# A two-layer decoder on one core: in both cross attentions the first eight heads' values and softmax denominators made by one product, and the first batches' expert slots counted on GpSimd

## The reference, cut to what matters

```python
x = x + L0_attn(layernorm(x))                          # banded self attention
x = x + L0_xattn(layernorm(x), ctx, ctx)               # cross attention, biases    <- changed
x = x + L0_ffn(layernorm(x))                           # 8 experts, top 2
x = x + L1_attn(layernorm(x) * gamma + beta)           # self attention, heads of 64
x = x + L1_xattn(ctx, ctx, layernorm(x))               # cross attention            <- changed
x = x + L1_ffn(layernorm(x))                           # 8 experts, top 2

# a cross attention, per batch and head:
scores = q @ k.T * scale          # 256 x 77
attn = softmax(scores, axis=-1)
out = attn @ v                    # 256 x 16
y = concat_heads(out) @ wo.T + bo
```

## Time and profile before

| | |
|---|---|
| median of 3 runs | 1504.77 us (1500.16 to 1508.09) |
| profiled execution | 1504.03 us, span 1502.4 us |
| granted TensorE clock, mean | 0.993 |
| TensorE busy | 1433.9 us, 95% of the span |
| VectorE busy | 748.7 us, 50% |
| ScalarE busy | 619.1 us, 41% |
| GpSimd busy | 490.5 us, 33% |
| stretch of L0x / L1x units | about 226 to 356 us / 1078 to 1213 us |

### The profile page before, as it was taken

The page is one execution under the profiler, slowest core; times in us unless marked ns, Lnnn a source line. Parts: engine busy times, 40 slices in busy tenths (PEclk is TensorE's granted clock), DMA queues, the critical chain, the costliest instruction groups (busy, mean ns, idle before and its releaser), DMA issues. The chain is left out here.

```text
span 1502.4 us, 34667 instructions
## 1 busy us (share of the span) xinstructions
PE 1433.9 (95%) x11880; PEld 1159.7 (77%) x11881; DVE 748.7 (50%) x2160; ACT 619.1 (41%) x1711; POOL 490.5 (33%) x758
## 2 busy tenths in 40 slices
PE   7999998988999999999999999999899899999998
PEld 5676766767899999976777777777666579999997
DVE  6666757887433333344444444444278862222222
ACT  2433346653222222235445444545366533333332
POOL 3545442444322122223233233333224452222222
PEclk9999999999999999999999999999999999999999
DMA  9920000152243434120000000000001522533332
GB/s 316 333 69 2 2 2 9 45 176 62 50 119 67 144 71 114 32 64 1 0 1 1 1 1 1 1 1 0 1 16 44 174 78 40 149 93 94 94 90 34
DMA packets 79666, 97.46 MB, mean 65 GB/s; under 512 B 10523, under 2 KB 72579, under 8 KB 79555
## 3 DMA queue, kind: packets, MB, share of 16 engines
q1 hardware_dynamic: 64643, 77.58, 16.4%
q0 software_dynamic: 13680, 17.19, 6.6%
q10 hardware_dynamic: 1232, 1.18, 0.2%
HBM read 57.51 MB, written 39.59 MB: 65 GB/s over the span
## 5 line engine op out<-in xcount | busy, mean ns | idle before, releaser
L1741 POOL TENSOR_TENSOR L1a_prob<-L1a_prob,L1a_rtot 128x1024 f32<-128x1024 f32 x64 | 121.1, 1892 | 275.8 <-DVE L1a_rtot L1614 275.8
L2270 PEld LDWEIGHTS L0x_ps<-L0f_rows_t,L0f_w_up 128*128 128x128 f32 x1584 | 183.7, 193 | 10.4 <-issue 9.0
L2270 PE MATMUL L0x_ps<-L0f_rows_t,L0f_w_up 128*128 128x128 f32 x1584 | 185.8, 277 | 5.6 <-issue 4.8
L2346 ACT ACTIVATE L1f_hid<-L1x_ps,L1f_b_up 128x128 f32<-128x128 f32 x296 | 92.4, 363 | 163.0 <-PE L1x_ps L2270 159.7
L2270 PEld LDWEIGHTS L1x_ps<-L1f_rows_t,L1f_w_up 128*128 128x128 f32 x1184 | 139.5, 194 | 3.4 <-issue 1.6
L2270 PE MATMUL L1x_ps<-L1f_rows_t,L1f_w_up 128*128 128x128 f32 x1184 | 140.4, 277 | 0.6 <-ACT L1f_rows_t L2330 0.6
L2279 PE MATMUL L1x_ps<-L1f_w_down,L1f_hid 128*128 128x256 f32 x592 | 134.1, 380 | 1.9 <-issue 1.9
L2214 POOL TENSOR_TENSOR turn<-eps 128x1 f32<-128x1 f32 x74 | 13.6, 184 | 372.3 <-DVE wv L2448 367.7
L1683 ACT ACTIVATE L1a_prob<-L1a_ps_s,L1a_nmax 128x256 f32<-128x256 f32 x256 | 118.2, 473 | 38.1 <-DVE L1a_nmax L1609 38.1
L2279 PEld LDWEIGHTS L1x_ps<-L1f_w_down,L1f_hid 128*128 128x128 f32 x592 | 109.6, 190 | 15.5 <-issue 2.1
L1245 POOL TENSOR_SCALAR_AFFINE_SELECT L0a_prob<-L0a_prob 128x128 f32<-128x128 f32 (+1 forms) x256 | 79.8, 353 | 104.3 <-ACT L0a_prob L1199 104.3
(11 more groups left out here) (486 smaller groups left out, 2812.5 us busy)
## 6 DMA issues: line engine op xcount, KB each, us to landing
expert_table<-zero SPq DMA_DIRECT2D x1, 16640.0 KB, 68.5
L0f_w_up<-in_w_dram SPq DMA_DIRECT2D x8, 1408.0 KB, 6.8
L1f_w_up<-in_w_dram SPq DMA_DIRECT2D x8, 1024.0 KB
L1f_w_down<-in_w_dram SPq DMA_DIRECT2D x8, 1024.0 KB
L0f_w_down<-in_w_dram SPq DMA_DIRECT2D x8, 768.0 KB, 8.7
L1f_rows<-expert_table SPq DMA_DIRECT2D x35, 130.0 KB
L0f_rows<-expert_table SPq DMA_DIRECT2D x32, 130.0 KB
sums<-X SPq DMA_DIRECT2D x8, 256.0 KB
```

Source lines behind the costliest of these rows:

```text
L1741: eng.tensor_tensor(v, v, r.unsqueeze(2).to_broadcast([P, 2 * QT_N, S]), ALU.mult).then_inc(norm_done, 1)
L2270: ins = eng.matmul(ps_h[c][:, o:o + P], w_up[par][:, t, w0:w0 + P], rows_t[:, t, :], start=(t == 0), stop=(t == DT - 1))
L2346: ins = eng.activation(hid[:, c, k * P:(k + 1) * P], ps_h[c][:, k * P:(k + 1) * P], ACT.Gelu, bias=b_up[par][:, 2 * c + k:2 * c + k + 1])
```

## The change

In both cross attentions:

- The tile v_s of an even unit (heads 0 to 7) now holds a value in every even column and a one in every odd column, so one product of 32 columns gives a head's values and its denominator in alternate rows. Each half of the heads goes to its own half of ps_o. Odd units (heads 8 to 15) keep two sets of products, with zeros in place of the ones and half_ones laid out to match.
- The even unit's ps_o is copied to SBUF by ScalarE (`gather`, tile gathered). SyncE brings rows together by four transfers within SBUF a batch (`move`: two for the sums, then two for the values). VectorE takes the reciprocal in SBUF (`sums_first`) and GpSimd multiplies (`first_outputs`).
- `slots` is split: `gates` stays on VectorE, the rest of the first five batches goes to GpSimd, written as `slots` there; the last three batches keep the old `slots` on VectorE.
- VectorE's `sums` of the odd unit runs ahead of the ordering of the experts, and waits of odds, choose and send are adapted.
- The first two weight loads are issued by ScalarE, one at the end of unit 11, one at the end of unit 12, and no longer by SyncE.
- Weights wo and bias bv are permuted on the host to the new order of rows.

```diff
             b = t[1]
-            eng.wait_ge(v_cleared, b % 2 + 1)
+            eng.wait_ge(v_cleared, 2 * (b % 2 + 1))
...
-            ins = eng.activation(even_odd(v_s[b % 2][0:SC, :, :]), bank[0:SC, 0:D].rearrange("p (a two d) -> p a two d", two=2, d=DH), ACT.Copy)
+            ins = eng.activation(v_s[b % 2][0:SC, :, 0::2], bank[0:SC, 0:D].rearrange("p (h d) -> p h d", d=DH), ACT.Copy)
...
+                def move(b):
+                    eng.wait_ge(copied, b + 1)
+                    if b:
+                        eng.wait_ge(rsum_done, b)
+                    for w in range(HALVES):
+                        eng.dma_start(summed_t[1 - w::2, :], gathered[w::2, w, :]).then_inc(sums_moved, 16)
+                    if b:
+                        eng.wait_ge(first_out, b)
+                    for w in range(HALVES):
+                        eng.dma_start(valued_t[1 - w::2, :], gathered[1 - w::2, w, :]).then_inc(values_moved, 16)
+
+                move(0)
                 for b in range(B):
+                    if b + 1 < B:
+                        move(b + 1)
                     eng.wait_ge(added, b + 1)
...
-                    if b == ORDER_BY + 1:
-                        experts["first_loads"](eng)
...
+                def sums_first(b):
+                    eng.wait_ge(sums_moved, 32 * (b + 1))
+                    if b:
+                        eng.wait_ge(first_out, b)
+                    eng.reciprocal(rsum_first[:, :], summed_t[:, :]).then_inc(rsum_done, 1)
...
                     if c == 0:
+                        if b:
+                            sums_first(b - 1)
                         if b + 2 < B:
                             first["statistics"](eng, b + 2)
                         if b >= 3:
-                            slots(b - 3)
+                            gates(b - 3)
+                        if b:
+                            sums(u - 1)
+                        if b >= 3:
+                            if b == 3 and not final or b - 3 == ORDER_BY or b - 3 in FULL_BY:
+                                eng.wait_ge(slot_done, b - 2)
...
-                    if u and u < units - 1:
-                        sums(u - 1)
...
+                def gather(b):
+                    eng.wait_ge(values_done, CHUNKS * b + 1)
...
+                    eng.activation(gathered, ps_o[:, :].rearrange("p (w s) -> p w s", w=HALVES), ACT.Copy).then_inc(copied, 1)
...
                     for r in range(GROUPS):
                         exponential(u, r)
+                    if c == 1:
+                        gather(b)
...
+                    for e in range(2):
+                        if u == 2 * (ORDER_BY + 3) + 1 + e:
+                            experts["first_load"](eng, e)
...
+                def first_outputs(b):
+                    eng.wait_ge(values_moved, 32 * (b + 1))
+                    eng.wait_ge(rsum_done, b + 1)
+                    if b:
+                        eng.wait_ge(projected, b)
+                    eng.tensor_tensor(o_t[:, 0, :], valued_t, rsum_first, ALU.mult).then_inc(first_out, 1)
...
                     if c == 0:
+                        if b:
+                            first_outputs(b - 1)
                         if b + 2 < B:
                             first["spread_norm"](eng, b + 2)
                         if b >= 3:
+                            slots(b - 3)
                             send(b - 3)
...
-                    if u:
-                        eng.wait_ge(o_out, u)
-                    for summed in range(2):
+                    flat = v_s[b % 2][0:SC, :, :].rearrange("p h n -> p (h n)")
+                    if c == 1:
+                        eng.wait_ge(copied, b + 1)
+                    elif b:
+                        eng.wait_ge(o_out, b)
+                    for summed in range(c + 1):
                         for w in range(HALVES):
                             for r in range(GROUPS):
-                                lhs = half_ones[0:SC, w, :] if summed else v_s[b % 2][0:SC, c * 8 + 2 * r + 1 - w, :]
+                                o = (summed if c else w) * S
+                                n = 2 * DH * (c * 8 + 2 * r + 1 - w) - (1 - w)
+                                lhs = half_ones[0:SC, w, :] if summed else flat[:, n:n + 2 * DH]
```

More of the change, by code:

```diff
@@ L138, in batches_of @@
         return b0, b1, b1 - b0
-    def even_odd(v):
-        return v.rearrange("p (a two) (half d) -> p a (two half) d", two=2, half=2)[:, :, 0::3, :]
     def weights_in(eng):
@@ L579, in _ @@
                             choose(b - 2)
-                        if u == units - 1:
-                            sums(u - 1)
                         if b >= 1:
                             add(b - 1)
-                    if u and u < units - 1:
-                        sums(u - 1)
                 slots(B - 3)
+                sums_first(B - 1)
                 x["take_early"](0)
```

77 lines of the change are left out of this document (56 added, 21 removed).

## The result

The changed kernel takes 1526.76 us (median of 3 runs, 1525.22 to 1527.20) against 1504.77: ratio 1.0147, 95% interval 1.0102 to 1.0191. It is slower by 22 us where 8.0 us less were forecast. Two views of the profiled execution come first: the head of its page, and three lines of its lists of instructions and transfers.

A forecast was written before the change was run, and what follows sets the result against it. TensorE was taken as the bound in most batches, with VectorE and the chain behind it stepping in at a few waits. Terms gave 4.8 us (L0x) plus 3.2 (L1x), together 8.0: 1504.0 to 1496.0 us, range 1484 to 1510.

The forecast's parts named there:

- TensorE is the bound: Both attentions: TensorE goes from product to product in most batches; removing one group per batch gives at most 14.9 us.
- the four waits that it names: TensorE's waits for o_t (twice), shifted queries and router's rows xr: 6.9 us in L0x, 5.7 in L1x.
- the router's chain has no room: Units 10 and 11 of L1x: TensorE reaches L804 at s+18.9, just as ScalarE's xr (ended s+18.5) is ready.
- the four batches from 3 on: Units 8 to 14: removed products and old waits against 6.8 us of new waits, net gain 2.2 (L0x), 1.0 us (L1x).
- The first three batches: Start of each attention, no sends, GpSimd has room: 2.8 us less a third, so 1.9 us gained.
- The slots on GpSimd: GpSimd ahead of sends, bias and router's norm: nine instructions, 2.4 us, delaying the router's rows.
- waits for xr: TensorE at L804, units 8, 10, 12, 14: new waits of 2.4, 0, 2.4 and 2.0, 6.8 us an attention.
- The relief every other batch: Units 8, 10, 12: a batch stretched by 2.4 us gives the next chain that time, so the next waits for nothing.
- The rival that the sums' transfers meet the weight loads: Units 10 and 12: sums land beside 2 MB loads, sums_first 4.2 us late, TensorE stands 2.7; 1515 us, chance 0.20.
- the prediction's sign of being wrong upwards: VectorE's wait at sums_first over 4 us in units 12 and 14 would show the prediction wrong upwards.
- The shared port: VectorE and GpSimd exclude each other in SBUF: added stalls from first_outputs and slots, one removed by moving bias; left at zero.
- The last unit: TensorE's 1.6 us wait for o_t of unit 14 gives way to ScalarE's copy: 1.5 us gained an attention.

The follow-up runs named there:

- e12: The kernel before without the second group of eight products of each even unit from the second batch on, nothing in their place: 1496.75 us, ratio 0.9929.
- e10: The changed kernel with each even unit's group of eight products issued twice, so TensorE has its old work again: 1526.68 us, ratio 1.0142.
- e6: e4 with the first two weight loads issued only in units 12 and 14, behind the transfers' landing: 1517.91 us, ratio 1.0070.
- e4: The changed kernel with GpSimd's bias of a batch put behind the router's norm of the batch before: 1513.63 us, ratio 1.0099.
- e5: The kernel before with six more activations on ScalarE, making the router's rows xr late once in each attention: 1520.57 us, ratio 1.0141.

## Why the prediction was wrong

**The bound (wrong reading of "TensorE is the bound").** That TensorE went from product to product was read as a ceiling of 14.9 us. The reading was too simple even for the kernel before: beside the four waits that it names, TensorE has others over 0.3 us, so that those come to 10.5 us in L0x and 9.4 in L1x, not 6.9 and 5.7. e12 gives -0.9 us in the stretches for 13.0 us of products, e10 nothing that can be told for 14.9. The prediction itself said that the router's chain has no room, and it counted the products of the four batches from 3 on as nearly nothing (2.2 and 1.0 us net). With three batches ahead of them that makes seven; the eighth batch's group is in no term, 0.93 us an attention. The first three batches, with no sends, did give something: the scores behind unit 5 start 0.8 us earlier in L0x (277.69 - 226.04 = 51.7 us from the first product before, 276.90 - 226.01 = 50.9 after) and 1.5 us earlier in L1x (55.6 and 54.1), where 1.9 was forecast.

**The slots on GpSimd (right in place and about in size).** 2.3 us for the nine instructions (277.00 to 279.24) against 2.4; waits for xr of 5.7 and 9.6 us against 6.8 each. The relief every other batch came in L0x (nothing, 2.4, 0.7 and 2.6 us in units 8, 10, 12 and 14) and not in L1x (1.0, 2.4, 1.8, 4.4), where the last had been taken as 2.0. That one is mis-sized: ScalarE waited there for the rows sent two batches earlier, 5.0 us after the last of their issues, and the prediction had put 3.6 us on such a landing and taken 2.0.

**The failing step: the waits were priced at their own length.** No term of the sum held TensorE's clock. A wait of 2.4 us was set against 2.4 us of products; waits of that kind were followed by up to 13.7 us at half clock (1214.9 to 1228.6 in L1x). The 18.8 us that the profiled execution lost so, against before, stand beside a loss of 21.1. Another way to the same share: over 25 executions of before on one chip the span was longer by 12 us for each hundredth of mean granted clock (1500.5 us at 0.995, 1514.7 at 0.984); the changed kernel's 0.980 against 0.993 is then 16 us. The third is the balance of busy time, 22.7 us. So 16 to 23 us are clock. Without it the three ways leave between 5 us lost and 2 us gained, where 8.0 us of gain were forecast: the waits net of the products were mis-sized too, by 6 us or more. The parts of this that can be named are the two waits of L0x that no term held, 2.7 and 2.3 us, and the waits for xr of L1x, 2.8 us over their 6.8. A range is all that can be given: while the clock is low other waits shrink.

The kernel before had the sign in its own trace, behind the wait for o_t in the last unit of L1x: the same sixteen products that take 1.07 us in the earlier trace rows take 1.93 us here.

```profile
1209.05 1.93 PE L865 MATMUL L1x_ps_o<-L1x_prob,L1x_v_s 77*32 77x256 f32 x16 [1.62 <-DVE L1x_o_t L483]
```

**The rival that the sums' transfers meet the weight loads (right in mechanism, small in price).** VectorE stood 4.9 and 4.2 us in unit 12 (forecast by that rival 4.2 us late), TensorE 2.0 us for o_t in L0x and not at all in L1x. e6 shows that the loads cause it. In unit 14 VectorE stood 5.0 and 5.9 us, so the prediction's sign of being wrong upwards (over 4 us in units 12 and 14) was met in both attentions; but in unit 14 the transfers were late by their place in SyncE's list, which no rival named. The argument against it was the Trainium skill, page "DMA: Bandwidth & Descriptors", section "Queues, rings and completion order", which says that the engines take queues in turn, packet by packet. From it the prediction drew that a short transfer would not stand behind the loads of another queue. The trace disagrees with that conclusion: 325.68 to 333.07 us beside the loads. It does not show in what turn the queues were served. That rival's time of 1515 was on the right side for a reason that holds only in part.

**The shared port (put at zero, not zero).** 1.98 us of VectorE in unit 7 became a wait of 2.74 us for TensorE, and the clock fell at its end (0.50 from 286.5 to 293.3). That is the rule of the page "SBUF — State Buffer" in the Trainium skill, section "Who interferes with whom", and the trace agrees; the prediction had it in its first half and let the second go. e4 moves the bias and takes 1.8 us of that wait away. first_outputs, too, held up a product of VectorE (0.63 us beside GpSimd's 0.73 at 334.97).

**The last unit.** The 1.6 us wait for o_t went, 0.9 us for ScalarE's copy came. Right in kind, half in size: 0.7 against 1.5 us.

## What to carry to other kernels

Before a microsecond of TensorE is counted as saved, ask what operand the next product waits for; if that chain has no room, the saving is a wait, and a wait on a busy TensorE can cost several times its length in clock. Read the granted clock of the kernel before in windows first, and price a new wait with e5's kind of test: one delay, put into the old kernel by hand, tells what such a wait costs. And when small transfers join a stage, look at what the queues beside them issue in the same microsecond, and at what the instruction ahead of them in their own issuer's list waits for.

## What the hardware showed that was not expected

- Two waits of 3.8 us cost 20.8 us (e5). At each the granted clock falls to 0.50, for 10.2 us in L0x (310.4 to 320.6) and 13.6 in L1x (1174.0 to 1187.6), although TensorE is busy for 4.00 of 4.00 us in the last two windows shown. TensorE's idle time did not rise; its products took 15.1 us longer.
- Waits of one length come with and without the fall: 2.43 us in unit 10 of L0x without, 2.42 us in unit 10 of L1x with it, in the same execution; 1.17 us without in the kernel before, 1.13 us at the same place with it in e5. What decides between them stays open.
- The kernel before scatters by 14 us on one chip, and its mean clock with it (0.984 to 0.995); on another it is 17 us, and 0.981 to 0.994.
- A transfer of 64 KB within SBUF lands 1.9 us after its issue in the median (below: size in KB, us to landing), and over 6 us after it (two issued from 325.7 to 326.8, landed by 333.1) beside 2 MB from DRAM on another queue.

```profile
wo<-wk SPq DMA_DIRECT2D x64, 64.0 KB, 1.9
```
